# Attention and feed-forward on one core: the output weight is turned by TensorE instead of by transposing DMAs, its row sums are taken earlier, and the first values are grown inside the second score product

## The reference

```python
x = x + xattn(layernorm(x), ctx_512, Wq, Wkv_expand, Wout)
x = x + ffn(layernorm(x), ffn_weight)

# xattn
qp = q @ Wq.T
k, v = split(latent_kv @ Wkv_expand.T, 2)
scores = einsum(qh, kh) / 8, masked causally, softmax      # per head
out = (attn @ vh).reshape(b, sq, H)
return out @ Wout.T
# ffn: x and weight quantised to e4m3 by their largest magnitudes, product cast to bf16
```

## Time and profile before

| what | value |
|---|---|
| median of 3 runs | 1764.5 us (1764.05 to 1764.87) |
| the profiled execution's own time | 1764.4 us |
| its span | 1762.6 us |
| PE busy | 1705.4 us (97%) |
| DVE busy | 1336.2 us (76%) |
| ACT busy | 680.0 us (39%) |
| POOL busy | 182.8 us (10%) |
| DMA | 269.39 MB, mean 153 GB/s |

### The profile page before, as it was taken

The page is one execution under the profiler, slowest core; times in us unless marked ns, Lnnn a source line. Parts: engine busy times, 40 slices in busy tenths (PEclk is TensorE's granted clock), DMA queues, the critical chain, the costliest instruction groups (busy, mean ns, idle before and its releaser), DMA issues.

```text
span 1762.6 us, 27918 instructions
## 1 busy us (share of the span) xinstructions
PE 1705.4 (97%) x11462; PEld 808.2 (46%) x11487; DVE 1336.2 (76%) x1914; ACT 680.0 (39%) x643; POOL 182.8 (10%) x141
## 2 busy tenths in 40 slices
PE   8759999999999999999999999999999999799998
PEld 4324454445444544454445444544444444444444
DVE  8856678778876787778777877887788666877775
ACT  5622233223322332233223322332233221699996
POOL 0000000000000000000000000000000002255555
PEclk9979999999999999999999999999999999999999
DMA  9645644554455445554455455544454543899995
GB/s 346 149 108 125 173 122 109 136 126 119 102 141 130 109 104 130 132 125 102 122 134 126 109 120 128 126 118 120 120 126 115 125 108 96 282 315 324 319 316 179
DMA packets 398437, 269.39 MB, mean 153 GB/s; under 512 B 350336, under 2 KB 352896, under 8 KB 398080
## 3 DMA queue, kind: packets, MB, share of 16 engines
q1 hardware_dynamic: 398336, 267.96, 57.3%
HBM read 117.44 MB, written 71.30 MB: 107 GB/s over the span
## 4 chain that ended last, share of the span: by engine, by line
PE 84%; DVE 10%; ACT 4%; issue 2%; DMA 1%; SPq 0%; DVEq 0%; ACTq 0%
PE ps_all L693 34%; PE ps_all L709 32%; PE ps_all L856 12%; DVE m_buf L1204 3%; PE ps_all L681 3%; PE ps_all L663 1%; PE ps_all L718 1%; DVE n_buf L1198 1%; DVE tile_space L1273 1%; DVE hsum L1267 1%; DVE tile_space L1261 1%; ACT tile_space L952 1%; PE ps_all L788 1%; ACT tile_space L956 1%; DVE hmax L1256 1%
## 5 line engine op out<-in xcount | busy, mean ns | idle before, releaser
L693 PE MATMUL ps_all<-m_buf,tile_space 128*128 128x504 f16 x3072 | 669.4, 377 | 4.3 <-DVE tile_space L1261 4.2
L709 PE MATMUL ps_all<-n_buf,tile_space 128*128 128x512 f16 x3024 | 669.1, 380 | 0.0
L693 PEld LDWEIGHTS ps_all<-m_buf,tile_space 128*128 128x128 f16 x3072 | 298.3, 98 | 357.9 <-issue 13.3
L709 PEld LDWEIGHTS ps_all<-n_buf,tile_space 128*128 128x128 f16 x3024 | 293.7, 98 | 357.7 <-issue 10.1
L960 ACT ACTIVATE tile_space<-tile_space,neg_mean 128x1024 f32<-128x1024 f32 x63 | 72.4, 1149 | 322.2 <-DVE neg_mean L1293 322.2
L555 POOL TENSOR_TENSOR rstd_x<-veps_x,minus_half 128x1 f32<-128x1 f32 x64 | 35.4, 553 | 1422.5 <-DVE veps_x L1228 1422.5
L956 ACT ACTIVATE tile_space<-tile_space,score_scale 128x1024 f32<-128x1024 f32 x64 | 73.4, 1147 | 244.3 <-DVE tile_space L1261 243.4
L952 ACT ACTIVATE tile_space<-tile_space 128x1024 f16<-128x1024 f32 x64 | 67.6, 1057 | 194.0 <-DVE tile_space L1273 194.0
L1215 DVE SCALAR_TENSOR_TENSOR tile_space<-tile_space 128x1024 f16<-128x1024 f32 x64 | 78.4, 1225 | 70.7 <-ACT tile_space L952 70.7
L1267 DVE TENSOR_REDUCE hsum<-tile_space 128x16 f32<-128x1024 f32 x64 | 77.9, 1217 | 58.4 <-ACT tile_space L956 58.4
L856 PE MATMUL ps_all<-wo_t,tile_space 128*128 128x512 bf16 x512 | 119.7, 382 | 2.4 <-DVE tile_space L1576 1.2
(11 more groups left out here) (147 smaller groups left out, 1507.4 us busy)
## 6 DMA issues: line engine op xcount, KB each, us to landing
tile_space<-in_x_dram SPq DMA_DIRECT2D x128, 512.0 KB, 4.0
x_scratch<-tile_space SPq DMA_DIRECT2D x64, 512.0 KB, 3.1
m_buf<-x_scratch SPq DMA_DIRECT2D x32, 512.0 KB, 5.4
tile_space<-x_scratch SPq DMA_DIRECT2D x32, 512.0 KB, 5.7
out_dram<-m_buf SPq DMA_DIRECT2D x32, 512.0 KB, 4.4
out_dram<-tile_space SPq DMA_DIRECT2D x31, 512.0 KB, 4.3
m_buf<-in_L_xattn_Wq_dram SPq DMA_DIRECT2D x4, 1024.0 KB, 12.0
n_buf<-in_L_xattn_Wout_dram SPq DMA_DIRECT2D x2, 2048.0 KB, 14.9
```

Source lines behind the costliest of these rows:

```text
L693: mm = nc.tensor.matmul(ps_s[:, half * HALF:half * HALF + RH], left[:, ls, c * P:(c + 1) * P], m_buf[:, rs, c, half * RH:(half + 1) * RH], ...
L709: mm = nc.tensor.matmul(to[:, cols], left[:, ls, j * P:(j + 1) * P], right[:, rs, j, cols], start=(c == 0 and i == 0), stop=(c == CT - 1 a ...
```

## The change

Four things are done together.
- **The output weight is turned by PE as it was loaded.** `turn_wout(j)` is now a PE function: 8 f32 transposes of 128x128 from `wout_f` into one of `ps_o`, `ps_p`, `ps_x`. Three are placed right behind the scores of tile 0, five between the chunks of the scores of tile 1. The eight transposing DMAs, their semaphore and SP's waits for them are gone.
- **It is split from PSUM.** `split_wout_hi` and `split_wout_lo` read the turned block in PSUM and write `wo_t` directly.
- **The row sums come earlier.** `Wout` is loaded by four DMAs of 1 MB; two sums stand before `copy_wkv(7, 2)`, one behind the third query-weight split, the others among the value splits and the first three `take_m`. The peak is turned at chunk 2 and not 5, and DVE's order around it changes with it.
- **The values are grown inside the second score product.** Pairs 0 and 1 are called behind chunks 6 and 8 of the scores of tile 1; ACT and DVE take blocks 0 and 1 at the head of step 0, and `maxima(1)` and `exponentials(1)` move behind blocks 2 and 3. Blocks 6 and 7 are taken before the probabilities of tile 1.

```diff
-        wout_split = [tile_space[:, i, :].bitcast(F16) for i in (11, 6, 7)] + [
-            flat(n_buf)[:, a * 2048:(a + 1) * 2048] for a in range(CT - 3)]
...
-        unread = [tile_space[:, i, :] for i in (12, 7, 6)]
-        wo_blocks = wo_t[:].rearrange("p s j c -> p (s j) c")
+        unread = [tile_space[:, i, :] for i in (12, 7)]
...
-        PEAKS_AT = 5
+        PEAKS_AT = 2
+        WOUT_PS = [(ps_o, ps_p, ps_x)[i] for i in (0, 1, 2, 0, 1, 2, 1, 0)]
+        WOUT_AT = {1: 3, 2: 4, 3: 5, 4: 6, 5: 7}
+        FIRST_PAIR_AT, SECOND_PAIR_AT = 6, 8
...
-            for i in range(2):
-                half = slice(4 * i, 4 * i + 4)
-                sp.dma_start(wout_f[:, half, :], wout_rows[:, half, :]).then_inc(got_wout[i], 16)
+            for i in range(4):
+                quarter = slice(2 * i, 2 * i + 2)
+                sp.dma_start(wout_f[:, quarter, :], wout_rows[:, quarter, :]).then_inc(got_wout[i], 16)
...
-
-            def turn_wout(a):
-                sp.wait_ge(wout_lo, a + 1)
-                sp.dma_start_transpose(wo_blocks[:, :, a * P:(a + 1) * P], wout_split[a]).then_inc(wout_turned, 16)
 
...
             load_x(xr, got_xr, 0, 0)
-            for a in range(4):
-                turn_wout(a)
             sp.wait_ge(p_lo, 1)
             turn_p(0, 0)
-            for a in range(4, CT):
-                turn_wout(a)
 
...
+            WOUT_FREE = ((peak_read, 4), (grow_free[0], 4), (grow_free[1], 4), (wout_lo, 1), (wout_lo, 2),
+                         (wout_lo, 3), (wout_lo, 5), (wout_lo, 4))
+
+            def turn_wout(j):
+                pe.wait_ge(got_wout[3], 16)
+                pe.wait_ge(*WOUT_FREE[j])
+                for a in range(CT):
+                    mm = nc.tensor.transpose(WOUT_PS[j][:, a * P:(a + 1) * P], wout_f[:, a, j * P:(j + 1) * P], ident[:])
+                mm.then_inc(wout_full, 1)
+
             def make_n_pair(b, m):
+                if is_step(b, 0):
+                    pe.wait_ge(wout_lo, (7, 7, 7, 8)[m])
...
+                        if known and t == 0:
+                            if c in WOUT_AT:
+                                turn_wout(WOUT_AT[c])
+                            if c == FIRST_PAIR_AT:
+                                make_n_pair(0, 0)
+                            if c == SECOND_PAIR_AT:
+                                make_n_pair(0, 1)
...
                     if known and t == 0:
-                        pe.wait_ge(wout_turned, 16 * CT)
-                        make_n_pair(0, 0)
-                        make_n_pair(0, 1)
-                        pe.wait_ge(peak_read, 4)
+                        pe.wait_ge(wout_lo, CT)
...
             scores(xt_buf[0], ready=first_chunk)
+            for j in range(3):
+                turn_wout(j)
...
             def sum_wout(a):
-                act.wait_ge(got_wout[a // 4], 16)
-                if a == 2:
-                    act.wait_ge(wkv_sum, 1)
-                if a >= 3:
-                    act.wait_ge(wout_sum, a - 2)
-                nc.scalar.activation(unread[a % 3], wout_f[:, a, :], ACT.Abs, accum_out=peaks[:, a:a + 1]).then_inc(wout_sum, 1)
-
-            def split_wout_hi(a):
-                if a >= 3:
-                    act.wait_ge(wout_lo, a - 2)
-                nc.scalar.activation(wout_split[a][:, 0:H], wout_f[:, a, :], ACT.Copy,
-                                     scale=to_f16[:, 2:3]).then_inc(wout_hi, 1)
+                act.wait_ge(got_wout[a // 2], 16)
+                if a >= 2:
+                    act.wait_ge(wout_sum, a - 1)
+                nc.scalar.activation(unread[a % 2], wout_f[:, a, :], ACT.Abs, accum_out=peaks[:, a:a + 1]).then_inc(wout_sum, 1)
+
+            def split_wout_hi(j):
+                act.wait_ge(wout_full, j + 1)
+                nc.scalar.activation(wo_t[:, 0, j, :], WOUT_PS[j][:], ACT.Copy, scale=to_f16[:, 2:3]).then_inc(wout_hi, 1)
...
                 if first:
-                    exponentials(1)
+                    grow_n(0)
+                    grow_n(1)
...
                 if first:
-                    for c in range(4):
+                    grow_n(2)
+                    grow_n(3)
+                    exponentials(1)
+                    for c in range(4, CT):
                         grow_n(c)
...
+            sum_wout(0)
+            sum_wout(1)
             copy_wkv(7, 2)
             copy_wkv(8, 3)
             act.wait_ge(scales_made, 2)
             for i in range(3):
                 split_wq_hi(i)
+            sum_wout(2)
             act.wait_ge(scales_made, 3)
             split_v_hi(0)
             split_wq_hi(3)
-            for a in range(1, 4):
-                split_v_hi(a)
-                sum_wout(a - 1)
-            for c in range(4):
+            split_v_hi(1)
+            sum_wout(3)
+            split_v_hi(2)
+            sum_wout(4)
+            split_v_hi(3)
+            for c in range(3):
                 take_m(c, c // 2)
-                sum_wout(3 + c)
+                sum_wout(5 + c)
             x_high(1, 1)
-            take_m(4, 2)
-            sum_wout(7)
-            for c in range(5, CT):
+            for c in range(3, CT):
                 take_m(c, c // 2)
             act.wait_ge(scales_made, 4)
-            act.wait_ge(got_v, 128)
-            act.wait_ge(kv_stored, 128)
             split_wout_hi(0)
             split_wout_hi(1)
             exponentials(0)
-            split_wout_hi(2)
+            for j in range(2, 6):
+                split_wout_hi(j)
             p_high(0)
-            for a in range(3, CT):
-                split_wout_hi(a)
+            split_wout_hi(6)
+            split_wout_hi(7)
 
...
-            def split_wout_lo(a):
-                dve.wait_ge(wout_hi, a + 1)
-                nc.vector.scalar_tensor_tensor(out=wout_split[a][:, H:2 * H], in0=wout_f[:, a, :], scalar=to_f16[:, 2:3],
-                                               in1=wout_split[a][:, 0:H], op0=ALU.mult,
+            def split_wout_lo(j):
+                dve.wait_ge(wout_hi, j + 1)
+                nc.vector.scalar_tensor_tensor(out=wo_t[:, 1, j, :], in0=WOUT_PS[j][:], scalar=to_f16[:, 2:3],
+                                               in1=wo_t[:, 0, j, :], op0=ALU.mult,
                                                op1=ALU.subtract).then_inc(wout_lo, 1)
...
-                if first:
-                    maxima(1)
...
+                    maxima(1)
+                    grow_n(4)
+                    grow_n(5)
...
+                if first:
+                    grow_n(6)
+                    grow_n(7)
...
-                if first:
-                    for c in range(4, CT):
-                        grow_n(c)
...
             take_m(0, 0)
+            variance(1, 1)
             take_m(1, 0)
-            variance(1, 1)
+            normalise(1, 1)
             take_m(2, 1)
-            normalise(1, 1)
-            take_m(3, 1)
-            x_low(1, 1)
-            take_m(4, 2)
             dve.wait_ge(wout_sum, CT)
             then(nc.vector.tensor_reduce(small[:, 15:16], peaks[:, 0:8], AX.X, ALU.max))
             spread_peaks(3, small[:, 15:16])
-            take_m(5, 2)
-            take_m(6, 3)
+            x_low(1, 1)
+            take_m(3, 1)
+            take_m(4, 2)
             all_peaks(3, amax4_all[:, 2:3])
             powers(slice(2, 3), 4)
+            for c in range(5, CT):
+                take_m(c, c // 2)
...
                                          1.0 / (N_SCALE * P_SCALE), ALU.mult, ALU.mult))
-            take_m(7, 3)
             nc.vector.memset(wait_carrier[:], 0.0).then_inc(x1_ready, 1)
-            split_wout_lo(0)
             dve.wait_ge(kv_stored, 128)
             mask_scores(0)
             maxima(0, masks=1)
-            split_wout_lo(1)
-            split_wout_lo(2)
+            for j in range(3):
+                split_wout_lo(j)
             sums(0)
+            split_wout_lo(3)
+            split_wout_lo(4)
             probabilities(0)
-            split_wout_lo(3)
+            split_wout_lo(5)
             p_low(0)
-            for a in range(4, CT):
-                split_wout_lo(a)
+            split_wout_lo(6)
+            split_wout_lo(7)
```

More of the change, by code:

```diff
@@ L186, in xattn_ffn_kernel @@
         got_wq = [sem(f"got_wq{i}") for i in range(4)]
-        got_wout = [sem(f"got_wout{i}") for i in range(2)]
+        got_wout = [sem(f"got_wout{i}") for i in range(4)]
         turned = sem("turned")
@@ L199, in xattn_ffn_kernel @@
         wout_lo = sem("wout_lo")
-        wout_turned = sem("wout_turned")
+        wout_full = sem("wout_full")
         k_stored = sem("k_stored")
```

## The result

The changed kernel took 1747.47 us in the median (1747.12 to 1748.27, 4 runs) beside 1764.28 (1763.95 to 1764.87) for the kernel before: ratio 0.9905, 95% interval 0.9888 to 0.9922, 16.8 us faster. The forecast was 1748.9, with 1745.5 to 1753.5 as its range.

A forecast was written before the change was run, and what follows sets the result against it. PE bounds the kernel, so start-up gains pass through whole: tile 0's product ends at 111.7 instead of 127.31 us, 15.6 earlier; 1764.4 - 15.6 = 1748.8, plus 0.1 for the median, 1748.9 us, range 1745.5 to 1753.5.

The forecast's parts named there:

- What bounds it, and the sum: Start-up to the end of tile 0's product: PE waits for the turned output weight; product ends 15.6 us earlier.
- Early sums: ACT's sums before PE's first take: first weight quarter lands near 26.5, nothing stalls, 0.6 us gained (bounds 0 and 0.6).
- Transposes: 64 on PE at 0.12 us each; three blocks free inside the softmax-head wait, five between tile 1's score chunks; clock kept.
- the rival in which they do not hold it: Transposes do not hold PE's clock, so tile 1's scores pay 1.4 us again: 1750.3; chance 0.14, shared with loss ahead of pair 1.
- The window that the prediction leaned on: 25.60 to 30.20 us before: 2.26 us of transposes alone on PE, granted clock 1.00, taken as showing the clock is kept.
- Splits, and DVE as what sets the path: DVE's eight low splits and tile 0's softmax run without a hole from 71.6 to 85.0 us; PE waits for DVE.
- The clock behind the holes: PE's clock drops ahead of pair 3 after 3.1 us idle, 8.4 us to product end; no drop ahead of pair 1.
- no drop ahead of pair 3: Case where PE's clock stays up ahead of pair 3, giving 1.7 us back: 1747.2 us; chance 0.14.
- lost ahead of pair 1: Case of a clock drop after 2.2 us of idle PE: pair takes 2.79, 1.3 us lost; 0.14 together with transposes not holding the clock.
- the forecast's own case: Whole kernel at 1748.9 us, within 1747.9 to 1749.9; chance 0.50.
- the allowance for semaphores: 0.2 us added to the end of tile 0's product for semaphores between engines, making 111.5 into 111.7.
- The shift passed on to the end: Behind 127 us PE has no slack, so the start-up's gain is passed on one to one to the span's end.

The follow-up runs named there:

- half_turned: Kernel before without the last four turning DMAs of the output weight, zeros standing for their part, so its output differs: 1756.73 us.
- late_sums: Changed kernel with the early sums undone: ACT's row sums and DVE's order as before, peak turned at chunk 5: 1749.88 us.
- after_again: The changed kernel itself, unaltered, run and profiled once more: 1748.59 us (1746.33 to 1748.92).
- idle_gap: Changed kernel with the first three blocks of transposes moved behind the wait for the softmax head, leaving PE idle between the two score products: 1753.14 us.
- sums_alone: Kernel before with only the four 1 MB loads, early row sums, DVE's order around them and peak at chunk 2; weight still turned by DMAs: 1762.74 us.
- keep_busy: Changed kernel with unread identity transposes filling three PE holes: 16 ahead of the scores of tile 0, 20 ahead of pair 1, 22 ahead of pair 3: 1746.13 us.
- exp_behind: Changed kernel with ACT's exponentials of tile 1 moved behind the high parts of blocks 4 and 5 of N: 1746.46 us.
- norm_behind: Changed kernel with DVE's takes of blocks 0 and 1 of N moved ahead of the normalising of tile 2: 1747.08 us.
- all_three: Changed kernel with both queue-order changes (ACT's exponentials, DVE's normalising) and three PE holes filled by 16, 8 and 6 transposes: 1742.98 us.
- four_holes: Changed kernel with both queue-order changes, three filled holes and a fourth filling around the turned peak of the query weight: 1742.37 us, ratio to before 0.9874.
- late_pairs: Changed kernel with pairs 0 and 1 of N put back behind the second score product: 1752.08 us (1748.53 to 1752.34).

## Why the prediction was right, and where it was off

**What bounds it, and the sum.** Right. The steps against the trace after: scores of tile 0 to end at 67.5, measured 63.08 + 4.00 = 67.1; scores of tile 1 to start at 71.7, 71.32; pair 1 at 90.7, 90.20; pair 3 at 103.1, 103.05; product to end at 111.7, 109.82. The hole's cause is shown by half_turned: with four DMAs fewer PE grows pair 0 at 88.28 and not at 98.86 us, and comes 7.6 us earlier to pair 1 and to all that follows.

**Early sums.** Right in kind, and the 0.6 is there (late_sums, and the idle 2.30 against 2.89). It was not all: the prediction had PE without another wait up to the end of the scores of tile 0, but the last chunk had waited for the last take of M, and the earlier peak gave back 0.25 us there. The landing came at 26.1, not 26.5. The last key split had ended 0.8 us earlier than before in this execution, at 25.96, so the sum waited 0.2; in after_again it did not wait.

**Transposes.** 24 took 2.78 us, 8 took 1.04: the 0.12 us of the earlier trace rows. They kept the clock: 1.00 from 66.90 to 86.00, where idle_gap without them shows 0.65 behind the hole. In all nine profiles that have 24 of them between the two score products, the first six matmuls behind took 1.44 us; in all four without them (before, half_turned, sums_alone, idle_gap) the clock fell. So the rival in which they do not hold it is refuted. In keep_busy nothing but such transposes stood in the 2.35 us ahead of pair 1, and the clock stayed at 1.00. The Trainium skill's rule behind that rival ("TensorE: Matmul & The Clock Gate", Part 4: PE-mode transpose), that a transpose does not count as work for the clock gate, does not hold for these f32 transposes. Its 275 ns for one is not found either: 0.12 us for f32 here. The window that the prediction leaned on, from 25.60 us, was weaker support than it looked. The same transposes around the same hole ran at a clock of 0.78 to 0.88 in five of the twelve profiles where that hole is not filled.

**Splits, and DVE as what sets the path.** Right: 14.44 of 14.70 us busy. exp_behind and norm_behind show it by moving nothing but queue order: 2.0 us, and 1.5 us ahead of pair 1.

**The clock behind the holes.** This is the term that was off. The prediction let the clock fall ahead of pair 3 and not ahead of pair 1. It was the other way round: pair 1 took 2.20 us at a clock of 0.58, pair 3 took 1.49 at 1.00. The 8.4 us from pair 3 to the end were 6.77: 1.6 us better. The reason given for pair 1 was that 2.2 us of idle time is shorter than any stretch with the lower clock behind it. Its shortest row was 2.89 us. In the profile after, a hole of 2.30 us ahead of 49.57 has a clock of 0.62 behind it, and the hole ahead of pair 1 itself became 2.63.

The end of the product came at 109.8 us where 111.7 was worked out. Of these 1.9 us, 1.6 are the clock ahead of pair 3, 0.5 are pair 1 coming earlier and 0.2 the allowance for semaphores, and the stretch from pair 1 to pair 3 took 0.45 more than forecast. Then 0.6 was lost near 1505 us. So the number lies near 1747.2, the case "no drop ahead of pair 3" with its chance of 0.14, and the case "lost ahead of pair 1" happened as well; that they nearly cancel the other small terms is luck. The forecast's own range, 1747.9 to 1749.9, missed the 1747.47 and holds the 1748.59 of after_again. A lottery of that size belonged into the range as what it is, and the chance of the forecast's own case was too high.

**The shift passed on to the end.** Right up to 1476 us. 0.6 us were lost behind it to the clock, which the prediction did not have.

**What was not seen ahead.** Without the first three blocks in the wait for the softmax head pair 1 comes 4.1 us later (idle_gap), cover and clock together, since DVE has no time to spare and waits for the first blocks itself. The code around 25 us has a hole after which the clock falls in some executions (five of the twelve profiles without a filling there), and costs 0.9 to 1.8 us.

## What to carry to other kernels

When a transfer is taken off the path, read which queue stands right behind it: here the hole alone was worth 7.6 us, and most of the other ten lie where DVE and ACT have another order of work or less to wait for. On an engine that has become the bound, the next gains are in the order of its queue, found by asking for each hole what was put ahead of the instruction that ends it. In a start-up full of short holes compare kernels by place in the timeline, not by medians alone, or fill the holes first, so that the clock is the same in both.

## What the runs showed of the hardware

A hole in TensorE's work can cost twice, and between 2.3 and 3.1 us its length did not say whether it would. Holes of 2.30 and 2.63 us were followed by mean granted clocks of 0.62 and 0.58 (1.2 GHz for most of the stretch), one of 2.87 us in the same execution by 1.00. The same 2.87 us hole was followed by the lower clock in late_sums and late_pairs. One such drop cost 0.7 us ahead of pair 1, where a wait behind it took part of it up, and 1.6 us ahead of pair 3.

f32 transposes of 128x128 that nobody reads held the clock at 1.00 (2.4 GHz) through each hole they filled, in keep_busy, all_three and four_holes. They cost nothing ahead of pair 1 in keep_busy: 18.9 us from the second score product to pair 1, with the 20 transposes and without.
